# Linear attention stage of a decoder: two buffers for state, queries, normalised and transposed tile, with the normalisation on ScalarE

## What is computed

```python
def _l2norm(t):
    n = jnp.linalg.norm(t, axis=-1, keepdims=True)
    return t / jnp.maximum(n, 1e-12)
q = _l2norm(proj(Wq)); k = _l2norm(proj(Wk)); v = proj(Wv)
v = v / jnp.power(jnp.float32(C), jax.nn.sigmoid(norm_const))
kv = jnp.einsum('nhcd,nhce->nhde', k, v)
attn = jnp.einsum('nhcd,nhde->nhce', q, kv)
out = attn.transpose(0, 2, 1, 3).reshape(N, C, d)
return out @ Wo.T
```

## Time and profile before

| what | value |
|---|---|
| median of the runs | 1883.64 us |
| the profiled execution's own time | 1881.6 us |
| its span, first to last instruction | 1879.7 us |
| PE busy in the span | 1665.8 us (89%) |
| DVE busy | 1366.1 us (73%) |
| ACT busy | 1280.1 us (68%) |
| POOL busy | 892.8 us (47%) |
| linear attention: first statistics, last addition | 9.7 us, 229.9 us |

### The profile page before, as it was taken

One profiled execution on the slowest core, in us unless ns is written; L12 is line 12 of the kernel. 1 busy time (PEld: TensorE's weight loads), 2 busy tenths in 40 slices (PEclk: granted clock), 3 DMA queues, 4 the chain that ended last, 5 costly groups with the idle time before them and its releaser, 6 DMA issues. The chain is left out here.

```text
span 1879.7 us, 50106 instructions
## 1 busy us (share of the span) xinstructions
PE 1665.8 (89%) x12187; PEld 1357.1 (72%) x12188; DVE 1366.1 (73%) x4364; ACT 1280.1 (68%) x3518; POOL 892.8 (47%) x2322
## 2 busy tenths in 40 slices
PE   5777769999998799996999999969999999659997
PEld 3444448888887344444888888858888888559997
DVE  5777658887786788884878777759888888624443
ACT  4444448888886678775888888759888888413332
POOL 1222135555552343342555555346788888624443
PEclk9999969999999899997999999979999999879999
DMA  8970000000000000000000000000111111047775
GB/s 226 403 302 0 0 11 13 13 12 12 13 13 6 1 0 0 0 0 1 1 0 0 0 0 0 1 21 25 29 34 33 34 33 34 27 138 235 236 229 159
DMA packets 85175, 107.73 MB, mean 57 GB/s; under 512 B 33682, under 2 KB 62501, under 8 KB 85102
## 3 DMA queue, kind: packets, MB, share of 16 engines
q1 hardware_dynamic: 80494, 98.01, 16.6%
q0 software_dynamic: 4320, 8.53, 1.3%
q10 hardware_dynamic: 288, 0.34, 0.1%
HBM read 63.18 MB, written 44.12 MB: 57 GB/s over the span
## 5 line engine op out<-in xcount | busy, mean ns | idle before, releaser
L1059 PE MATMUL xa_ps_o<-xa_vb,xa_pt 128*128 128x96 f32 x2048 | 246.3, 273 | 0.0
L1059 PEld LDWEIGHTS xa_ps_o<-xa_vb,xa_pt 128*128 128x128 f32 x2048 | 239.0, 192 | 0.1
L902 ACT ACTIVATE xa_pt<-xa_ps_pt 128x512 f32<-128x512 f32 x256 | 139.1, 594 | 81.2 <-PE xa_ps_pt L976 81.0
L714 DVE TENSOR_REDUCE xa_mx<-xa_ps_s 128x8 f32<-128x512 f32 x256 | 164.8, 685 | 19.8 <-PE xa_ps_s L994 15.9
L1236 PE MATMUL ffn_ps_h<-w1t,ffn_xdt 128*128 128x512 f32 x384 | 176.6, 596 | 0.0
L866 POOL TENSOR_TENSOR xa_km<-xa_kt,const_sb 128x256 f32<-128x256 f32 x256 | 152.8, 618 | 33.5 <-ACT xa_kt L915 28.5
L720 DVE TENSOR_TENSOR xa_pr<-xa_ps_s,xa_mx 128x512 f32<-128x512 f32 x256 | 163.6, 679 | 0.2
L896 ACT ACTIVATE xa_pr<-xa_pr 128x512 f32<-128x512 f32 x256 | 147.2, 622 | 4.2 <-DVE xa_pr L720 1.4
L994 PE MATMUL xa_ps_s<-xa_km,xa_qm 64*128 64x256 f32 x1024 | 143.5, 399 | 4.0 <-POOL xa_km L866 4.0
L976 PEld LDWEIGHTS xa_ps_pt<-const_sb,xa_pr 128*128 128x128 f32 x1024 | 110.8, 142 | 41.4 <-issue 40.8
L976 PE MATMUL xa_ps_pt<-const_sb,xa_pr 128*128 128x128 f32 x1024 | 140.7, 281 | 0.0
(11 more groups left out here) (286 smaller groups left out, 4762.3 us busy)
## 6 DMA issues: line engine op xcount, KB each, us to landing
exp_w1b<-in_L_ffn_w_dram SPq DMA_DIRECT2D x71, 512.0 KB, 3.7
x_sorted<-no_row SPq DMA_DIRECT2D x1, 34320.0 KB, 92.4
xa_cn<-in_ctx_dram SPq DMA_DIRECT2D x128, 64.0 KB, 1.8
exp_xg<-x_sorted SPq DMA_DIRECT2D x71, 66.0 KB, 2.5
xa_mi<-in_mask_BxSxS_ik_dram SPq DMA_DIRECT2D x128, 32.0 KB
out_dram<-exp_y,exp_token POOLq DMA_INDIRECT x71
x_sorted<-x_sb,place POOLq DMA_INDIRECT x64, 2.4
x_sb<-in_x_dram SPq DMA_DIRECT2D x1, 512.0 KB, 5.0
```

Of the source, the lines that this page charges most:

```text
L714: nc.vector.tensor_reduce(mx[:, 8 * hf:8 * hf + 8], scores_of(hf), axis=AX.X, op=ALU.max).then_inc(s["max_done"], 1)
L902: nc.scalar.activation(pt[:, 512 * hf:512 * hf + 512], ps_pt[hf][:, :], ACT.Copy).then_inc(s["pt_sb"], 1)
L1059: last = nc.tensor.matmul(ps_o[:, 2 * VW * g:2 * VW * g + av_w], pt[:, P * g:P * g + P], vb[(r + 1) % RING][:, 2 * VW * g:2 * VW * g + av_ ...
```

## The change

All of it lies in `linear_attention`. `xn`, `xt`, `qt` and `kvm` get two buffers each, and the guards that protected the single buffers are eased by one tile. The normalisation moves from DVE to ACT (`Identity` with a scale and a bias by row), for which POOL makes `shift` with two more instructions. The statistics run one tile further ahead (t+7). `floored` goes: its maximum becomes a minimum with 1e12 inside the instruction that makes `qk`, now a scalar-tensor-tensor one. PE's transpose of `xn` stands first in its turn, ACT's `xn` and `xt` first in ACT's; DVE's `inv` moves to the head of the next turn, and the addition ahead of `ss`. The diff leaves out only blank lines and the file's untouched parts:

```diff
--- before.py
+++ after.py
@@ -430,16 +424,18 @@
         def ps(name, w=512):
             return ctx.enter_context(nc.psum_tensor("lin_ps_" + name, [P, w], F32))
         ln = layernorm_memory(nc, k, ctx, "lin")
-        xn, xt = sb("xn", [P, D]), sb("xt", [P, P])
-        sq, ss, length = sb("sq", [P, 256]), sb("sum_sq", [P, 32]), sb("length", [P, 32])
-        floored, inv = sb("floored", [P, 32]), sb("inv_length", [P, 32])
+        xn = [sb(f"xn{i}", [P, D]) for i in range(2)]
+        xt = [sb(f"xt{i}", [P, P]) for i in range(2)]
+        shift, minus = sb("ln_shift", [P, 1]), sb("ln_minus", [P, 2])
+        sq, ss, length, inv = sb("sq", [P, 256]), sb("sum_sq", [P, 32]), sb("length", [P, 32]), sb("inv_length", [P, 32])
         qk = [sb(f"qk{i}", [P, 256]) for i in range(2)]
         v = [sb(f"v{i}", [P, 2, D]) for i in range(2)]
-        qt = sb("qt", [P, 3, S])
-        kvm, at = sb("kvm", [P, 2, D]), sb("at", [P, P])
+        qt = [sb(f"qt{i}", [P, 3, S]) for i in range(2)]
+        kvm = [sb(f"kvm{i}", [P, 2, D]) for i in range(2)]
+        at = sb("at", [P, P])
         ps_qkv = [ps("qkv0"), ps("qkv1")]
         ps_xt, ps_kv, ps_qt, ps_at, ps_y = (ps(n) for n in ("xt", "kv", "qt", "at", "y"))
-        names = ["consts", "xt_done", "xt_sb", "qkv_done", "sq", "ss", "length", "floored", "inv", "qk", "v_sb",
+        names = ["consts", "product", "shift", "xt_done", "xt_sb", "qkv_done", "sq", "ss", "length", "inv", "qk", "v_sb",
                  "kv_done", "kvm", "qt_sb", "at_done", "at_sb", "y_done", "x_done"]
         s = {n: k.sem("lin_" + n) for n in names}
         nt = k.nt
@@ -455,52 +451,50 @@
 
             @block.vector
             def _(dve):
+                nc.vector.memset(ln["eps"][:, :], LN_EPS)
+                nc.vector.memset(ln["half"][:, :], -0.5)
+                nc.vector.memset(minus[:, 0:1], -1.0)
                 for q in range(2):
                     nc.vector.memset(v[q][:, :, :], 0.0)
-                nc.vector.memset(qt[:, :, :], 0.0)
-                nc.vector.memset(ln["eps"][:, :], LN_EPS)
-                nc.vector.memset(ln["half"][:, :], -0.5).then_inc(s["consts"], 1)
-
+                    last = nc.vector.memset(qt[q][:, :, :], 0.0)
+                last.then_inc(s["consts"], 1)
                 dve.wait_ge(k.x_in, 16)
 
                 def body(t, q):
                     if isinstance(t, int) and t == 0:
                         dve.wait_ge(k.x_rest, 16)
-                    if live(t + 6):
-                        layernorm_stats(nc, dve, k, t + 6, ln)
-                        dve.wait_ge(ln["stats"], t + 7)
+                    if live(t + 7):
+                        layernorm_stats(nc, dve, k, t + 7, ln)
+                        dve.wait_ge(ln["stats"], t + 8)
+                        wait(dve, s["shift"], t + 7)
+                    if live(t + 3):
+                        dve.wait_ge(s["length"], t + 4)
+                        wait(dve, s["qk"], t + 3)
+                        nc.vector.reciprocal(inv[:, :], length[:, :]).then_inc(s["inv"], 1)
+                    if live(t + 7):
+                        layernorm_var(nc, ln)
                     if live(t + 3):
                         dve.wait_ge(s["inv"], t + 4)
                         wait(dve, s["kv_done"], t + 2)
-                        nc.vector.tensor_tensor(qk[1 - q][:, :].rearrange("p (g d) -> p g d", d=HD),
-                                                ps_qkv[1 - q][:, 0:256].rearrange("p (g d) -> p g d", d=HD),
-                                                inv[:, :].unsqueeze(2).broadcast_to([P, 32, HD]), ALU.mult).then_inc(s["qk"], 1)
-                    if live(t + 6):
-                        layernorm_var(nc, ln)
+                        nc.vector.scalar_tensor_tensor(qk[1 - q][:, :].rearrange("p (g d) -> p g d", d=HD),
+                                                       inv[:, :].unsqueeze(2).broadcast_to([P, 32, HD]), 1.0 / L2_EPS,
+                                                       ps_qkv[1 - q][:, 0:256].rearrange("p (g d) -> p g d", d=HD),
+                                                       ALU.min, ALU.mult).then_inc(s["qk"], 1)
                     if live(t + 2):
                         dve.wait_ge(s["kv_done"], t + 3)
-                        wait(dve, s["at_done"], t + 2)
-                        nc.vector.tensor_tensor(kvm[:, :, :], ps_kv[:, 0:2 * D].rearrange("p (b c) -> p b c", b=2),
+                        wait(dve, s["at_done"], t + 1)
+                        nc.vector.tensor_tensor(kvm[q][:, :, :], ps_kv[:, 0:2 * D].rearrange("p (b c) -> p b c", b=2),
                                                 k.blk[:, :].unsqueeze(1).broadcast_to([P, 2, P]), ALU.mult).then_inc(s["kvm"], 1)
+                    if live(t):
+                        dve.wait_ge(s["y_done"], t + 1)
+                        xs = k.x[:, col(t), :].rearrange("p a d -> p (a d)")
+                        nc.vector.tensor_tensor(xs, xs, ps_y[:, 0:D], ALU.add).then_inc(s["x_done"], 1)
                     if live(t + 4):
                         dve.wait_ge(s["sq"], t + 5)
                         wait(dve, s["length"], t + 4)
                         nc.vector.tensor_reduce(ss[:, :], sq[:, :].rearrange("p (g d) -> p g d", d=HD), axis=AX.X,
                                                 op=ALU.add).then_inc(s["ss"], 1)
-                    if live(t + 6):
-                        wait(dve, s["xt_done"], t + 6)
-                        layernorm_scale(nc, dve, k, t + 6, ln, xn[:, :]).then_inc(ln["normed"], 1)
-                    if live(t):
-                        dve.wait_ge(s["y_done"], t + 1)
-                        xs = k.x[:, col(t), :].rearrange("p a d -> p (a d)")
-                        nc.vector.tensor_tensor(xs, xs, ps_y[:, 0:D], ALU.add).then_inc(s["x_done"], 1)
-                    if live(t + 4):
-                        dve.wait_ge(s["length"], t + 5)
-                        nc.vector.tensor_scalar(floored[:, :], length[:, :], L2_EPS, None, ALU.max).then_inc(s["floored"], 1)
-                        dve.wait_ge(s["floored"], t + 5)
-                        wait(dve, s["qk"], t + 4)
-                        nc.vector.reciprocal(inv[:, :], floored[:, :]).then_inc(s["inv"], 1)
-                pipeline_pairs(dve, nt, 6, body)
+                pipeline_pairs(dve, nt, 7, body)
                 dve.wait_ge(s["x_done"], nt)
 
             @block.gpsimd
@@ -508,19 +502,32 @@
                 pool.wait_ge(s["consts"], 1)
 
                 def body(t):
-                    if live(t + 6):
-                        layernorm_rstd(nc, pool, t + 6, ln)
-                pipeline(pool, nt, 6, body)
+                    if live(t + 7):
+                        layernorm_rstd(nc, pool, t + 7, ln)
+                        pool.wait_ge(ln["rstd"], t + 8)
+                        nc.gpsimd.tensor_tensor(minus[:, 1:2], ln["mv"][:, 0:1], ln["r"][:, :], ALU.mult).then_inc(s["product"], 1)
+                        pool.wait_ge(s["product"], t + 8)
+                        nc.gpsimd.tensor_tensor(shift[:, :], minus[:, 0:1], minus[:, 1:2], ALU.mult).then_inc(s["shift"], 1)
+                pipeline(pool, nt, 7, body)
 
             @block.scalar
             def _(act):
                 act.wait_ge(s["consts"], 1)
 
                 def body(t, q):
+                    if live(t + 6):
+                        act.wait_ge(s["shift"], t + 7)
+                        wait(act, s["xt_done"], t + 5)
+                        nc.scalar.activation(xn[q][:, :], k.x[:, col(t + 6), :].rearrange("p a d -> p (a d)"), ACT.Identity,
+                                             bias=shift[:, 0:1], scale=ln["r"][:, 0:1]).then_inc(ln["normed"], 1)
+                    if live(t + 5):
+                        act.wait_ge(s["xt_done"], t + 6)
+                        wait(act, s["qkv_done"], t + 4)
+                        nc.scalar.activation(xt[1 - q][:, :], ps_xt[:, 0:P], ACT.Copy).then_inc(s["xt_sb"], 1)
                     if live(t + 2):
                         act.wait_ge(s["kv_done"], t + 3)
-                        wait(act, s["at_done"], t + 2)
-                        nc.scalar.activation(qt[:, 0:3:2, :], ps_qt[:, 0:P].rearrange("p (b c) -> p b c", b=2),
+                        wait(act, s["at_done"], t + 1)
+                        nc.scalar.activation(qt[q][:, 0:3:2, :], ps_qt[:, 0:P].rearrange("p (b c) -> p b c", b=2),
                                              ACT.Copy).then_inc(s["qt_sb"], 1)
                     if live(t + 4):
                         act.wait_ge(s["qkv_done"], t + 5)
@@ -536,17 +543,17 @@
                         nc.scalar.activation(at[:, :], ps_at[:, 0:P], ACT.Copy).then_inc(s["at_sb"], 1)
                     if live(t + 4):
                         act.wait_ge(s["ss"], t + 5)
-                        wait(act, s["floored"], t + 4)
+                        wait(act, s["inv"], t + 4)
```

(21 more changed lines are left out.)

## The result

The kernel after the change takes 1815.48 us (median of 4 runs, 1814.36 to 1816.98); the kernel before, with a fourth run added to the three, 1881.97 us. The ratio is 0.9647, with a 95% interval of 0.9636 to 0.9659: 66.5 us less. Forecast were 1822 us with a range of 1813 to 1842, and faster with 0.95. The profiled execution took 1816.98 us, its span is 1815.1 us.

A forecast was written before the change was run, and what follows sets the result against it. A 3.31 us ACT-PE ring was taken to bound the linear stage, then PE at 2.13 plus 0.11 us. 61 turns by 1.04, less 1.5, saves 61.9 from 1881.6; plus 2.0 for the median, 1822 us, range 1813 to 1842.

The forecast's parts named there:

- the ring of 3.31 us: Linear stage's turn: 1.59 us of ACT, 1.58 of PE and two hand-overs, closed by single buffers; the change opens it.
- 1.5 us net: Fill and drain of the linear stage: late first `shift`, longer `xn`, earlier statistics; 1.5 us lost, between 0 and 3.3.
- Two signs: Profile signs for the linear stage: qkv starts 2.2 to 2.3 us apart, last addition near 168 us instead of 229.9.
- 61 turns by 1.04: Linear stage's gain: each of 61 turns 1.04 us shorter, 63.4 us, before 1.5 us of fill and drain.
- PE's sum of 2.13 us: PE's own work in a linear-stage turn, products and transposes added start to start: 2.13 us.
- I add the 0.11 us hand-over of that wait: PE's state product still waits for fresh `kvm` and `qk`; 0.11 us added, between 0 and 0.5, giving 2.24 a turn.
- So PE is the likely bound at 2.13 us: Linear stage after the change: PE's work limits the turn; a turn of 2.1 to 2.3 us had chance 0.57.
- the DVE ring: DVE's steps from `length` through `inv`, `qk`, `kvm`, addition and `ss`, plus hand-over: 2.01 us a turn, under PE's 2.13.
- The POOL-ACT ring: POOL's steps to `shift`, then ACT's `xn` and back, with hand-overs: 2.05 us a turn, under PE's 2.13.
- full durations: Rival, DVE takes the bound: without overlap of starts its ring is 2.39 us, total 1831 us; chance 0.18.
- POOL's `shift` at 0.40: Rival, POOL and ACT form the ring: new POOL steps at 0.40, turn 2.47 us, 1836; chance 0.20 including the mixture.
- A mixture of such waits that I have not found: Rival: unidentified waits make a linear-stage turn of 2.75 us, total 1853; chance 0.20 shared with POOL and ACT.

The follow-up runs named there:

- The swap: Changed kernel with DVE's two waits ahead of `inv` exchanged, the guard for `qk` first and the wait for `length` last: 1813.21 us, ratio 0.9622.
- the copy inside it: Changed kernel plus one spare DVE copy of 64 columns behind `kvm` in each turn: 1816.97 us, ratio 0.9650, mean turn 2.240 us.
- the transpose that cost PE 0.11 and the turn nothing: Changed kernel with PE's transpose of `xn` issued twice in each turn: 1816.77 us, ratio 0.9638, mean turn 2.164 us.
- two kernels with a part of the change missing: Kernel before with only two `qt` and `kvm`: 1859.03 us; changed kernel with the transpose of `xn` last in PE's turn: 1859.40 us.
- the ring of 2.80 us above: DVE and POOL ring, `mv` to `mv`, seen in the kernel before with only two buffers of `qt` and `kvm`: 1859.03 us, ratio 0.9861.
- the swap and the second buffers: Changed kernel with the waits ahead of `inv` exchanged and two buffers of `mv`, `r` and `shift`: 1810.50 us, ratio 0.9608.
- eight turns a round: Changed kernel with exchanged waits, two buffers of `mv`, `r` and `shift`, and all loops unrolled by 8 in place of 4: 1808.17 us, ratio 0.9606.

## Why the prediction was right, and where it was off

**Right:** the ring of 3.31 us was the bound and the change opened it; the wait for the attention product is gone, and comes back with single `qt` and `kvm`. The turn lies in the forecast's 2.1 to 2.3 us. `xn` on ACT lasts 0.49 us, `shift` 0.19, the stage's only table load stands ahead of the first `length`, as before (18.1 us, before 15.1), and the granted clock is 1.00. `qk` as a scalar-tensor-tensor instruction lasts 421 ns and costs nothing, as taken. Of the ends, 1.5 us net were forecast; they cost 3.2 less 1.9, 1.3 us. Two signs missed by the same error: qkv starts 2.13 us apart instead of 2.2 to 2.3, and the last addition is at 160.8 us instead of near 168.

**The sum:** 61 turns by 1.04 were forecast, 63.4 us; 63 turns between first and last qkv gave 70.1, 1.11 each. Two more turns are 2.2 us of the difference, the shorter turn 4.5. The stage gained 68.9 us where 61.9 were forecast; that the total comes nearer (66.5) is luck, since the later stages took longer, by 4.2 us in the profiled execution. The mis-sized term is PE's sum of 2.13 us, with the step "I add the 0.11 us hand-over of that wait" on top. PE's own work is 1.97, since two of its shares were read from the earlier trace rows behind a wait: qkv 0.75 instead of 0.65, the state product 0.50 instead of 0.43. For qkv the trace shows the weight load (PEld) starting with the product where PE has waited, and 0.11 us ahead of it (103.73 and 103.84) where it has not. Before, then after:

```profile
128.09 0.30 PEld L561 LDWEIGHTS lin_ps_qkv<-w_lin,lin_xt 128*128 128x128 f32 x2 [0.67 <-ACT lin_xt L544]
```

```profile
103.73 0.30 PEld L568 LDWEIGHTS lin_ps_qkv<-w_lin,lin_xt 128*128 128x128 f32 x2
```

Part of this came back at the loop's jump, which the sum had not: 2.164 in the mean over 2.13.

**The failed step** is the sentence "So PE is the likely bound at 2.13 us". The engine was wrong, and that its number, 2.13, is the measured steady turn is luck: PE's sum was 0.16 us too large and the DVE ring's 0.12 too small, and they met there. The DVE ring was forecast at 2.01, with 0.25 from `length` to its follower, taken from the earlier trace rows, where the follower was `floored`. With the statistics and further waits in front of `inv`, it is 0.43, and the ring 2.13. The swap showed that 0.07 of the difference of 0.18 is the order of the two waits; what the rest is was not separated. That this ring binds is shown by the copy inside it (0.10 more in a steady turn), the swap (0.07 less), the transpose that cost PE 0.11 and the turn nothing, and `xn` on DVE, 0.26 us of work placed in the wait for `length` that lengthened the steady turn by 0.03. The POOL-ACT ring was forecast at 2.05 and runs at 2.13 in the changed kernel, 2.07 with the swap: at 2.13 it has 0.06 us of slack at least.

**The rivals.** With full durations the DVE ring would have been 2.39 us. The overlap of the earlier trace rows stayed: `ss` at 103.23 lasts 0.41, and the statistics start at 103.56, 0.08 before its end. The Trainium skill ("VectorE: DVE Perf Modes", "The DRAIN you can't avoid") says that the next instruction does not start until the pipe is empty, and in the same paragraph that one which is not held starts earlier; the prediction took up only the first. Read as no start before the predecessor's recorded end, it does not hold for these pairs. POOL's `shift` at 0.40 did not come. "A mixture of such waits that I have not found", at 2.75 us, was real but lies beside the change: two kernels with a part of the change missing run at 2.915 and 2.850.

**What the parts are worth,** each taken back alone from the changed kernel, by the last addition: the place of the transpose 43.5 us, `qt` and `kvm` 36.2, `xn` and `xt` 9.9, the engine of `xn` 2.5. They sum to more than the 68.9 gained, so they are not independent: one ring can need several of them to be opened. The move of the normalisation to ACT, the largest edit of the change, is the least. What counts by the ring of 2.80 us above is that `xn` no longer stands in the turn of its own statistics, and the kernel with `xn` on DVE has that as well. Not taken back alone were the earlier statistics, the dropped `floored`, DVE's new order and ACT's; what they carry is not known.

## To carry to other kernels

Write out every ring that the single buffers close, PSUM tiles included, with the order of each engine's turn in it, before you split one: the gain of a second buffer is the distance to the next ring, and the next ring here lay at 2.80 us. When several rings end within 0.1 us of each other, a busy share of 99% names nothing; add a small piece of work to one engine, once inside and once outside its wait, and see which moves the turn. Put the wait that comes last at the end of a list of waits; it costs nothing, and here it gave 0.07 us a turn.

## What was not expected of the hardware

- A wait that was already met cost 0.07 us when it stood behind the binding one (`length` to `inv` 0.43 against 0.36, with and without the second buffers of `mv`, `r` and `shift`); ahead of `ss` no such cost shows (0.04 us from the squares' end).
- qkv held PE for 0.75 us from start to start behind a wait and for 0.65 without one, its duration 0.91 against 0.81. The state product held it for 0.50 to 0.51 behind a wait and for 0.43 without.
- The jump of the hardware loop shows as one ACT wait of some 0.3 us a round, and a turn 0.16 us longer in the changed kernel, 0.21 with the swap and the second buffers, 0.34 with eight turns a round.
